# The last normalisation of z: ScalarE in place of VectorE in a mixture of experts

## What is computed

```python
x = x + gnn(layernorm(x)) + mix(layernorm(x))
xn = layernorm(x)
w = softmax(xn @ Wr + br)                       # 8 weights for each token
h = relu(bn1(einsum('bfd,edh->bfeh', xn, W1) + b1))
h = relu(bn2(einsum('bfeh,ehk->bfek', h, W2) + b2))
y = einsum('bfeh,ehd->bfed', h, Wo) + bo
x = x + einsum('bfed,fe->bfd', y, w)
```

## Time and profile before

| | |
|---|---|
| time, median of 3 runs | 3786.02 us (3780.11 to 3786.73) |
| the profiled execution | 3781.71 us, span 3777.7 us |
| mean granted clock | 0.998 |
| TensorE busy | 3632.6 us, 96% |
| VectorE busy | 2105.0 us, 56% |
| ScalarE busy | 1418.3 us, 38% |
| GpSimd busy | 2754.5 us, 73% |
| affine on VectorE | 26 instructions, the first pair at 2954.4 us, the last from 3679.3 |

### The profile page before, as it was taken

One profiled execution on the slowest core, in us unless ns is written; L12 is line 12 of the kernel. 1 busy time (PEld: TensorE's weight loads), 2 busy tenths in 40 slices (PEclk: granted clock), 3 DMA queues, 4 the chain that ended last, 5 costly groups with the idle time before them and its releaser, 6 DMA issues.

```text
span 3777.7 us, 69343 instructions
## 1 busy us (share of the span) xinstructions
PE 3632.6 (96%) x26358; PEld 2033.9 (54%) x26358; DVE 2105.0 (56%) x6775; ACT 1418.3 (38%) x2665; POOL 2754.5 (73%) x2845
## 2 busy tenths in 40 slices
PE   2899999999999999999999999999999999999999
PEld 1455554644456555555556555555554556665666
DVE  9988775555465443732227222272223776777766
ACT  6666664200042000510006000060001767677777
POOL 5566664777767777667776777667776699999997
PEclk9999999999999999999999999999999999999999
DMA  6444342668525555255552565535554100000000
GB/s 206 146 124 150 125 153 84 206 222 279 171 99 189 192 177 173 86 186 193 196 179 99 166 210 179 165 135 193 190 177 126 55 22 12 23 12 23 11 16 10
DMA packets 203708, 506.20 MB, mean 134 GB/s; under 512 B 33860, under 2 KB 137872, under 8 KB 196848
## 3 DMA queue, kind: packets, MB, share of 16 engines
q0 software_dynamic: 83360, 227.95, 20.4%
q1 hardware_dynamic: 120016, 273.74, 20.0%
HBM read 412.08 MB, written 89.48 MB: 133 GB/s over the span
## 4 chain that ended last, share of the span: by engine, by line
PE 79%; DVE 9%; ACT 4%; issue 3%; POOL 2%; DMA 2%; POOLq 0%; SPq 0%; ACTq 0%; DVEq 0%
PE bank L1181 49%; PE bank L2428 6%; PE bank L2411 5%; PE bank L2396 5%; PE bank L1217 4%; PE bank L1293 3%; PE bank L983 2%; ACT h L2467 1%; DVE zh L2167 1%; ACT f L2468 1%; DVE st L2192 1%; DMA sg<-pieces_d,ssrc 1%; DVE ohk L782 1%; POOL ry L1406 1%; DVE ohl L781 1%
## 5 line engine op out<-in xcount | busy, mean ns | idle before, releaser
L1181 PE MATMUL bank<-slab,pieces 128*128 128x510 fp8e4 (+1 forms) x9408 | 2312.0, 378 | 5.1 <-DVE slab L801 5.1
L1518 POOL DMA_INDIRECT sg<-pieces_d,ssrc x1322 | 1257.2, 951 | 539.9 <-PE bank L1217 246.5
L1181 PEld LDWEIGHTS bank<-slab,pieces 128*128 128x128 f16 (+1 forms) x9408 | 800.6, 97 | 673.0 <-DVE slab L801 7.5
L1899 DVE TENSOR_SCALAR so<-iota,skey 128x49 f16<-128x49 f16 (+21 forms) x1322 | 315.0, 258 | 608.3 <-PE bank L1217 605.4
L1423 ACT ACTIVATE z<-bank,prm,ct 128x510 f32<-128x510 f32 (+2 forms) x130 | 95.0, 750 | 1229.9 <-DVE st L1417 1229.9
L1217 PEld LDWEIGHTS bank<-so,sg 128*128 128x128 f16 x5288 | 322.3, 96 | 280.5 <-DMA sg<-pieces_d,ssrc 7.8
L1518 POOL DMA_INDIRECT sgm<-pieces_d,ssrc x400 | 381.4, 954 | 121.9 <-issue 88.4
L2686 POOL TENSOR_SCALAR btmp<-bob,rw 128x256 f32<-128x256 f32 (+1 forms) x343 | 400.7, 1168 | 33.5
L2467 ACT ACTIVATE h<-bank,fscale 128x512 f16<-128x512 f32 (+2 forms) x416 | 315.2, 758 | 186.4 <-PE bank L2411 186.2
L1217 PE MATMUL bank<-so,sg 128*128 128x51 f16 (+20 forms) x5288 | 343.0, 182 | 5.1 <-DMA sg<-pieces_d,ssrc 5.1
L930 ACT ACTIVATE slab<-bank 128x490 fp8e4<-128x490 f32 x408 | 278.6, 695 | 140.7 <-PE bank L983 137.1
(11 more groups left out here) (355 smaller groups left out, 3941.1 us busy)
## 6 DMA issues: line engine op xcount, KB each, us to landing
slab<-slabs SPq DMA_DIRECT2D x40, 3123.8 KB
pieces_d<-pieces SPq DMA_DIRECT2D x60, 512.0 KB
slabs<-slab SPq DMA_DIRECT2D x8, 3123.8 KB, 11.2
sg<-pieces_d,ssrc POOLq DMA_INDIRECT x1322
mx<-xnorm SPq DMA_DIRECT2D x24, 512.0 KB, 6.4
ws<-L_ffn_W_dram SPq DMA_DIRECT2D x32, 256.0 KB, 5.7
sgm<-pieces_d,ssrc POOLq DMA_INDIRECT x400
experts<-wp SPq DMA_DIRECT2D x24, 256.0 KB, 4.5
```

The lines of the kernel that those rows point to most:

```text
L1181: ins = pe.matmul(psD[half][:, 0:w], PC[:k, a, c:c + P], v[:k, a, :], start=(r == 0), stop=(r == 97))
L1518: pool.indirect_dma_start(out=SG[j % ring_of(l)][:, :], out_offset=None, in_=d_H[:, :], in_offset=bass.IndirectOffsetOnAxis(ap=SI[:, j:j + ...
L1899: dve.tensor_scalar(SO[j % ring_of(l)][:, 0:w], iota[:, 0:w], SK[:, j:j + 1], None, ALU.is_equal).then_inc(s_soh, 1)
```

## The change

From group 1 on, ScalarE applies the affine, with two Identity activations that have a and b as scale and bias, in place of two VectorE instructions. The place in the list is the same, but it is now ScalarE that comes to it in its own order. Group 0 stays on VectorE.

```diff
@@ act_ffn
                 act_hidden(h2, f2, psG, 1, e, m, n, s_2h, s_2f)
+            elif kind == "affine" and c:
+                act.wait_ge(s_gev, gemm_count(L - 1, 1, groups_to(c1), 1))
+                act.wait_ge(s_bn, norm_count(L - 1, 1))
+                for m in range(2):
+                    z = Z[:, m, c0:c1]
+                    ins = act.activation(z, z, ACT.Identity, bias=scaled[:, m, 1:2], scale=scaled[:, m, 0:1])
+                ins.then_inc(s_faff, 1)
             elif kind == "root":
@@ dve_ffn
-            elif kind == "affine":
+            elif kind == "affine" and c == 0:
                 dve.wait_ge(s_gev, gemm_count(L - 1, 1, groups_to(c1), 1))
                 for m in range(2):
                     z = Z[:, m, c0:c1]
```

## The result

The changed kernel takes 3791.02 us (median of 22 runs, 3785.15 to 3795.72); the kernel before, timed beside it on the same chip, takes 3783.39 us (22 runs, 3779.69 to 3787.03). The ratio is 1.0019, 95% interval 1.0013 to 1.0025: 7.2 us slower, between 4.9 and 9.5. The profiled execution of the changed kernel has 3788.9 us and a span of 3784.8, so 7.2 and 7.1 more than that of before. The forecast was 4.8 us more.

The account below looks back on a forecast made before the run. TensorE, busy 96% of the span, was taken as the bound. Late low halves cost 4.3 us in eight groups, 0.4 in group 11 and 0.0 in group 12: 4.8 more on 3786.0, giving 3790.8 us; range 3782 to 3797.

Parts of the forecast that it names:

- within 0.2%: Whole kernel: time changes by no more than 0.2% (7.6 us) either way; chance 0.72.
- its own marks: Groups 2 to 9, first expert: third product 3.5 us, sixth load waiting 0.8 to 0.9 us, group period 65.65.
- signs of being wrong: Mixture stage: period the same or less, sixth load's wait under 0.3 us, or low halves over 0.9 us there.
- TensorE is the bound, and an edit is worth what it does to its waits: Mixture stage: TensorE busy 64.89 of 65.10 us a group; VectorE or ScalarE edits count only through TensorE's waits.
- An Identity of 512 columns from SBUF takes 0.713 us from start to start: ScalarE's added affine: 0.713 us a start, bounded by 0.66 and 0.806, worked out from the 256-column norms.
- Rival 5: ScalarE: a table load before each Identity pair, 12 x 1.28, 15 us, 3806 us; chance 0.01.
- The f of half 1 comes 1.43 us later than without the pair, and the low half 0.54 later than before: Groups 3 to 10, first expert's second product: delayed f makes the third product's sixth load 0.54 us later, 4.3 us in all.
- rival 2: Late low half also meets GpSimd, 1.17 for 0.69 us at ten places: 9.6 us more, 3795.6; chance 0.15.
- Rival 1: First expert's second product: low half late by ScalarE's two instructions, 3789.8 to 3792.7 us; chance 0.60.
- Nothing else is late: High half, next second product, transposes, and groups 1 and 2 in ScalarE's idle time: no cost.
- Rival 3: Mixture stage: relief of VectorE and GpSimd gives the loss back elsewhere, about 3786 us, not slower; chance 0.18.
- Rival 4: Mixture bias: GpSimd, 6 us in hand, becomes the bound by losing 0.6 us a group, 3794 us; chance 0.03.

Follow-up runs that it names:

- the reduced GpSimd: Six of eight experts' mixture-bias terms left out of the kernel before, the changed one and the one with ScalarE's early affine: 4131.26, 4139.72 and 4134.01 us.
- the early place and relief: Kernel before, with affine of groups 3 to 12 on ScalarE ahead of second product half 0, and GpSimd's first mixture-bias term moved to ScalarE: 3785.64 us, ratio 1.0008.

## Why the prediction held, step by step

**The number.** 4.8 us more were forecast and 7.2 measured, and the time lies well inside the range. That the forecast of "within 0.2%" held is in part luck: the ratio is 1.0019 with an interval to 1.0025, and on the other chip it is 1.0023. By its own marks the prediction is right on the place, the wait and the direction, and short in the size: the third product has 3.87 us and not 3.5, its load waits 1.19 and not 0.8 to 0.9, the period is 65.96 and not 65.65. One of its signs of being wrong came true, a low half of over 0.9 us at that place. The steps tell which term was short.

**TensorE is the bound, and an edit is worth what it does to its waits.** Right. 17.9 us less on VectorE bought nothing, and the 7.5 us are in waits of TensorE: 12.8 against 4.8 for this low half. ScalarE's busy time rose by 14.7, less than VectorE's fell; "as much" was forecast.

**An Identity of 512 columns from SBUF takes 0.713 us from start to start.** Right: 0.70 to 0.71 from start to start, where one has a mean length of 0.815. It was worked out from four norms at 256 columns and the slope of h. The page "ScalarE: Activation LUTs" of the Trainium skill gives, in its section "What ACT_TABLE_LOAD costs", 186 ns for an activation, 93 for each pointer operand, 0.833 for a column and 93 of overlap with its neighbour. From this I estimate 0.706 us for two pointers and 512 columns; the trace agrees with its 0.70 to 0.71. Rival 5 is out: no table load stands between these instructions, and one in the whole stage as before.

**The f of half 1 comes 1.43 us later than without the pair, and the low half 0.54 later than before.** The first is right (1.41). The second fell short by a single term. From the start of that f to the end of its low half were to be 1.49 us; there are 1.83, because the low half takes 1.03 and not 0.69. So the load starts 0.87 later relative to the product and not 0.54: the 0.54 of the prediction and some 0.33 for the longer low half. That GpSimd makes it longer is shown by the run with GpSimd idle there: 0.69.

**This is rival 2, in part.** It had the mechanism, 1.17 in place of 0.69 at ten places. It took place in the eight regular groups with 0.34 in place of 0.48, and in group 10 with a low half of 1.24 (the group is longer by 0.75 where 0.44 was said). It did not in group 11, where the narrow low half has 0.56. The prediction gave this rival 0.15 and took the median of all 144 low halves as the price instead. The median is still near the least in the changed kernel, and that was the trap:

```profile
L2540 DVE TENSOR_TENSOR h<-f,h x144: 673/693/1172, 3025.6 to 3613.7; 128x512 f16<-128x512 f32 x144
```

A low half that sits in a pattern that repeats each group has one price in all of them, and the median over the 16 places of a group says nothing about that one. The trace of before has this on GpSimd here:

```profile
3226.23 0.85 POOL L2689 TENSOR_TENSOR mb<-mb,btmp 128x256 f32<-128x256 f32 x1
3227.18 1.24 POOL L2686 TENSOR_SCALAR btmp<-bob,rw 128x256 f32<-128x256 f32 x1
```

A low half moved to 3226.3 would have met at least one of them. That could have been read, and it would have raised rival 2's chance; its price it would not have given, since the edit moves GpSimd's instructions too. The measured sum: 8 x 0.85 + 0.75 + 0.0 = 7.5 us, of which the prediction's own mechanism is 4.8.

**Rival 1, the late f alone,** is confirmed where it can be seen alone: with the reduced GpSimd the third product takes 3.54 us, which is what the prediction says for it (3.00 + 0.54). The step "0.54 more" has in it that the kernel before already pays 0.22; with GpSimd idle at the place the change costs 0.76.

**Nothing else is late.** Right: the transposes, the next second product and the groups 0 and 1 cost nothing. In the run with groups 1 and 2 alone the period and the stage are those of before.

**Rival 3, relief of VectorE gives it back,** didn't show: the regular groups have no gain. Of the 12.3 us that the second product's loads waited for low halves, 11.5 are left. The page "SBUF — State Buffer" of the Trainium skill, section "SBUF: two separate sides", says that VectorE and GpSimd share a pair of ports, which an instruction that needs it holds for its whole length while the other engine's waits. The runs agree in so far as VectorE's instructions are longer beside GpSimd's: 1.69 against 1.00 for the pair, 1.03 to 1.24 against 0.69 for the low half, the first of each with the full and the second with the reduced GpSimd. They also show that this isn't the fate of every such instruction: the median is 0.69 with GpSimd at work all the time.

**Rival 4, GpSimd becomes the bound,** had a chance of 0.03 and didn't happen in the change; the margin is still 6.1 us. But it is what happened when the same pair was put early, with either engine: 0.9 to 2.0 us a group more on GpSimd, until nothing was left of the margin after five to seven groups. With relief of GpSimd, both reduced and moved to ScalarE, those waits were gone. The 6 us were not worn away before, since GpSimd's period was exactly TensorE's, 65.11 before and 65.96 after, although it waits for nobody in these groups.

**What stays open.** Why GpSimd needs 65.1 us a group in one order against VectorE and 66 to 67 in another; no run sets that phase by itself, and a count of who met whom was not made. Why the total with the early place and relief doesn't show the 1.4 us by which its stage is shorter. And whether a version with all the work can be faster than before: none was shown here.

## What to carry to other kernels

An engine with spare time isn't free at a particular moment of its queue: what counts is which instruction stands behind the new one and who waits for that. The place decided here. The same pair put earlier cost TensorE nothing at its place, on either engine, but the time was lost again elsewhere. Between the halves of the product it made the third product 0.76 us longer on ScalarE, with GpSimd out of the way, and behind the next product it made the transposes' load wait 0.73.

In a stage whose period repeats, price an instruction at its own place in the pattern and not by the median of its line, and keep both its short and its long price when the edit shifts it against an engine that was seen to stretch it. A constant margin of another engine need not be spare time: here it was a rhythm in step with TensorE's, and it was gone when the step changed. After an edit look at the margin group by group.

## What the runs showed of the hardware that was not expected

- A VectorE instruction has one length or another according to what GpSimd does beside it (0.69 or 1.03 us for the same low half, 1.00 or 1.69 for the pair), and small edits elsewhere change which places pay. Relieving GpSimd of one instruction in 15 of its bias work made the stage 5 us longer; taking six of eight terms away made it 6.1 us shorter (811.19 against 817.33 for the unchanged kernel on the same chip).
- GpSimd's own period for the same instructions was 65.1 us in one kernel and up to 67.1 in another, 3% more, with only the place of the pair changed.
- The same program took 3782 us on one chip, 4141 and 4178 on two others. For the one with 4141 all of it arose in the six layers (2954 against 3318 us); the stage behind them was the same within 0.7 us. The page has the DMA engines busy for 0.2 to 0.8 in nearly all slices of the layers, and a window of the stage for 0.05; that this is the reason was not tested.
- A weight load's wait isn't the product's loss: the load waits 1.19 us, the matmul behind it 0.91, and the product is longer by 1.09 than an unbroken one of 2.78.
